# Routed experts: the 48-row rests of the down products side by side in the array, in bursts of four tiles, with three tables of sums

## The reference

```python
# x: 1024 tokens x 256; 16 experts, 4 chosen per token, hidden width 176
shared = silu_and_mul(x @ shared_gate_up_w.T) @ shared_down_w.T   # hidden width 704
shared = shared * sigmoid(x @ sgate_w.T)
topk_w, topk_ids = top_k(softmax(x @ gate_w.T), 4)
for w13_e, w2_e, e in zip(w13, w2, range(16)):
    coef = sum(where(topk_ids == e, topk_w, 0))
    h = silu_and_mul(x @ w13_e.T)          # 256 -> 2 x 176 -> 176
    acc = acc + (h @ w2_e.T) * coef        # 176 -> 256, the down product
out = shared + acc
```

## Time and profile before

| | |
|---|---|
| median of 3 runs | 1252.41 us (1249.12 to 1254.31) |
| profiled execution | 1253.93 us, of which the span from first to last instruction is 1252.0 us |
| first routed stage, first to last up product | 425.11 to 539.58 us |
| second routed stage, the same | 1119.70 to 1233.52 us |
| PE busy | 94% of the span |
| granted TensorE clock, mean | 0.967 of full speed |

### The profile page before, as it was taken

The page is one execution under the profiler, slowest core; times in us unless marked ns, Lnnn a source line. Parts: engine busy times, 40 slices in busy tenths (PEclk is TensorE's granted clock), DMA queues, the critical chain, the costliest instruction groups (busy, mean ns, idle before and its releaser), DMA issues.

```text
span 1252.0 us, 23038 instructions
## 1 busy us (share of the span) xinstructions
PE 1175.0 (94%) x7484; PEld 1008.6 (81%) x7484; DVE 807.0 (64%) x2038; ACT 752.3 (60%) x1734; POOL 600.4 (48%) x497
## 2 busy tenths in 40 slices
PE   6999999999897899989999999999999989489997
PEld 5878888888784777768999999999999988377775
DVE  7766767777882433477777777777777787143335
ACT  5866667666551333427888887887888865033332
POOL 3211222121137165625776777677776643705663
PEclk9999999999997899989999999999999998789999
DMA  3366766653245777741322222232222015556665
GB/s 114 88 181 169 175 174 174 170 162 71 58 153 203 181 137 137 129 103 51 89 77 59 59 61 65 61 70 79 59 75 59 17 48 158 201 168 112 117 116 145
DMA packets 94277, 141.59 MB, mean 113 GB/s; under 512 B 8184, under 2 KB 73976, under 8 KB 93048
## 3 DMA queue, kind: packets, MB, share of 16 engines
q1 hardware_dynamic: 74400, 102.32, 29.8%
q0 software_dynamic: 15744, 20.98, 9.8%
q10 hardware_dynamic: 4056, 17.30, 4.6%
HBM read 99.71 MB, written 40.86 MB: 112 GB/s over the span
## 4 chain that ended last, share of the span: by engine, by line
PE 80%; DVE 6%; DMA 6%; issue 4%; ACT 2%; POOL 1%; SPq 0%; DVEq 0%; ACTq 0%; POOLq 0%
PE ps L276 20%; PE ps L278 19%; PE ps L277 19%; PE ps L1116 7%; PE ps L1141 5%; DMA sums_d<-e_y,xg 3%; PE ps L551 2%; DMA rows_a<-a_rows_d 1%; PE ps L1129 1%; PE ps L1093 1%; DVE valT L762 1%; PE ps L1680 1%; PE ps L565 1%; DMA a_vg_raw<-a_vg 1%; DVE x L1419 1%
## 5 line engine op out<-in xcount | busy, mean ns | idle before, releaser
L1291 POOL DMA_INDIRECT sums_d<-e_y,xg x88 | 137.6, 1564 | 137.2 <-ACT e_y L1218 79.8
L1116 PE MATMUL ps<-w,e_xT 128*128 (+1 forms) x376 | 127.2, 461 | 2.5 <-ACT e_xT L1201 1.7
L1412 DVE COPY e_hT<-ps 88x256 f32<-88x256 f32 x94 | 39.5, 420 | 132.0 <-PE ps L1129 118.0
L427 POOL TENSOR_TENSOR aw_lo<-aw_raw,aw_hi 128x512 fp32r<-128x512 f32 x32 | 42.0, 1317 | 152.5 <-ACT aw_hi L423 152.5
L276 PE MATMUL ps<-xn_hi,aw_hi 128*128 128x512 f32 x256 | 111.2, 434 | 2.7 <-DVE bmat_lo L790 2.7
L857 DVE TENSOR_TENSOR m_a<-ps,e_a 128x384 f32<-128x384 f32 x128 | 71.3, 557 | 58.5 <-PE ps L551 57.9
L278 PE MATMUL ps<-xn_hi,aw_lo 128*128 128x512 f32 x256 | 101.4, 396 | 0.0
L277 PE MATMUL ps<-xn_lo,aw_hi 128*128 128x512 f32 x256 | 100.9, 394 | 0.0
L1141 PE MATMUL ps<-w,e_hT 88*128 (+1 forms) x376 | 96.7, 379 | 0.0
L656 ACT COPY late<-ps 128x256 f32<-128x256 f32 x128 | 47.7, 373 | 69.7 <-PE ps L278 69.6
L427 POOL TENSOR_TENSOR ms_b_lo<-m_b,ms_b_hi 128x384 fp32r<-128x384 f32 x64 | 65.0, 1017 | 49.2 <-ACT ms_b_hi L423 49.2
(11 more groups left out here) (311 smaller groups left out, 4145.8 us busy)
## 6 DMA issues: line engine op xcount, KB each, us to landing
rows_a<-a_rows_d SPq DMA_DIRECT2D x64, 256.0 KB, 5.1
xg<-slots_d SPq DMA_DIRECT2D x94, 144.0 KB
slots_d<-slot_init SPq DMA_DIRECT2D x10, 1152.0 KB, 6.9
w<-moe_up ACTq DMA_DIRECT2D x8, 1408.0 KB
wconv_raw<-b_conv SPq DMA_DIRECT2D x16, 513.0 KB
aw_raw<-a_heads SPq DMA_DIRECT2D x32, 256.0 KB, 3.0
wvo_raw<-b_vo SPq DMA_DIRECT2D x16, 512.0 KB, 3.4
rows_b<-b_rows_d SPq DMA_DIRECT2D x32, 256.0 KB, 4.8
```

The source lines that it names most:

```text
L427: return nc.gpsimd.tensor_tensor(dst[1], src, f32(dst[0]), ALU.subtract).then_inc(sem(done_sem), 1)
L1116: ins = nc.tensor.matmul(ps[:, 2 + t % 2, 0:2 * E_HIDDEN], e_xT[:, t % 2, k], weights_of(w13, t, at_w, k * 2 * E_HIDDEN, 2 * E_HIDDEN), st ...
L1291: nc.gpsimd.indirect_dma_start(sums_d[f][t % CHAINS], bass.IndirectOffsetOnAxis(ap=xg[:, t % XG, ROW_ID:ROW_ID + 1].bitcast(U32), axis=0), ...
L1412: nc.vector.tensor_copy(e_hT[0:HALF_E, t % 2], ps[0:HALF_E, 4 + t % 2, 0:2 * P].rearrange("p (j m) -> p j m", j=2)).then_inc(sem("e_hT"), 1)
```

## The change

- The down product of a tile, 176 rows, is cut into 128 rows (`h_main`) and a rest of 48 (`h_rest`), where it was 88 and 88. The rest of an even tile lies on partitions 0 to 47, that of an odd tile on 64 to 111, so that both can stand in the array at once.
- Down products are no longer done tile by tile but in groups (`DOWN_GROUPS`): nine of four tiles, five of two, and one of one. A group does all its rests, then all its mains. In a group of four, two tiles share a PSUM bank, and one ACT copy takes both out.
- DVE copies the turned hidden values with two instructions, and copies the row numbers of each tile to `e_ids`, so that an `xg` buffer is free as soon as DVE and PE have read it.
- For odd tiles from 16 on, ACT first copies the rest of the down weights to a fixed place (`w_rest`), with a register load of its own.
- PE's register load for tile t+1 stands behind the up product of tile t.
- Three tables of sums instead of two, eight `e_y` buffers instead of four.
- The down weights are laid out on 128 partitions instead of 88.

```diff
+DOWN_GROUPS = [range(t, t + 4) for t in range(0, 36, 4)] + [range(t, t + 2) for t in range(36, TILES - 1, 2)] + [range(TILES - 1, TILES)]
+DOWN_LAG = 2
+E_REST, REST_AT = E_HIDDEN - P, P // 2
-XG, YS, CHAINS, W_GROUPS = 8, 4, 2, 4
+XG, YS, CHAINS, W_GROUPS, HT = 8, 8, 3, 4, 6
...
         def f_experts_pe(pe, f):
-            for t in range(-1, TILES + 2):
+            for t in range(-1, TILES + DOWN_LAG):
                 if t + 1 < TILES:
                     e_turn_pe(pe, f, t + 1)
                 if 0 <= t < TILES:
-                    if t >= EXPERTS:
-                        if t == EXPERTS:
+                    e_up_pe(pe, f, t, at_w)
+                    if EXPERTS <= t + 1 < TILES:
+                        if t + 1 == EXPERTS:
                             routed(pe, "dve", f, "w_at")
-                        at_w[t % 3] = pe.value_load(w_at_i[0:1, t - EXPERTS:t - EXPERTS + 1], min_val=0,
-                                                    max_val=(EXPERTS - 1) * E_STRIDE)
-                    e_up_pe(pe, f, t, at_w)
+                        at_w[t + 1] = expert_at(pe, t + 1)
                 if 0 <= t - 1 < TILES:
                     e_turn_h_pe(pe, f, t - 1)
-                if 0 <= t - 2:
-                    if t - 2 == TILES - 1:
+                for group in due(t):
+                    if group[-1] == TILES - 1:
                         e_last_pe(pe, f, 0)
-                    e_down_pe(pe, f, t - 2, at_w)
+                    e_down_pe(pe, f, group, at_w)
...
+            nc.tensor.transpose(ps[:, 4 + t % 2, 0:P], e_h[:, t % 2, 0:P], ident)
+            nc.tensor.transpose(ps[0:E_HIDDEN - REST_AT, 4 + t % 2, P:2 * P], e_h[:, t % 2, REST_AT:], ident
+                                ).then_inc(sem("e_turned_h"), 1)
...
+        def e_down_pe(pe, f, group, at_w):
+            pe.wait_ge(sem("e_hT"), TILES * f + group[-1] + 1)
+            if group[0] > 0:
+                pe.wait_ge(sem("e_y"), len(READY) * f + ready(group[0]))
...
+            for t in group:
+                r = rest_rows(t)
+                if t >= EXPERTS and t % 2:
+                    pe.wait_ge(sem("w_rest"), MORE_TILES // 2 * f + (t - EXPERTS) // 2 + 1)
+                    w = w_rest[r, t // 2 % (HT // 2)]
+                else:
+                    w = weights_of(w2[r], t, at_w, DM, DM)
+                nc.tensor.matmul(out_of(t, group), h_rest[r, t // 2 % (HT // 2)], w, start=t - group[0] < 2, stop=False,
+                                 skip_group_check=True)
+            for tiles in banks_of(group):
+                for t in tiles:
+                    ins = nc.tensor.matmul(out_of(t, group), h_main[:, t % HT], weights_of(w2, t, at_w, 0, DM),
+                                           start=False, stop=True, skip_group_check=True)
+                ins.then_inc(sem("e_down"), 1)
...
+        def e_rest_act(act, f, t):
+            r = rest_rows(t)
...
+            nc.scalar.copy(w_rest[r, t // 2 % (HT // 2)], w2[r, DM:][:, bass.ds(expert_at(act, t), DM)]).then_inc(sem("w_rest"), 1)
...
+            nc.scalar.copy(e_y[:, n % YS:n % YS + len(tiles)], ps[:, 6 + t % 2, 0:len(tiles) * DM].rearrange("p (i m) -> p i m", m=DM)
+                           ).then_inc(sem("e_y"), 1)
...
+            for n, t in enumerate(ORDER[:POOLED]):
+                pool.wait_ge(sem("e_y"), len(READY) * f + ready(t) + 1)
+                if n >= CHAINS:
+                    added(pool, f, n - CHAINS)
...
+            nc.vector.tensor_copy(e_ids[:, t:t + 1], xg[:, t % XG, ROW_ID:ROW_ID + 1].bitcast(U32)).then_inc(sem("e_row"), 1)
...
-            nc.vector.tensor_copy(e_hT[0:HALF_E, t % 2], ps[0:HALF_E, 4 + t % 2, 0:2 * P].rearrange("p (j m) -> p j m", j=2)
+            turned_h = ps[:, 4 + t % 2, :]
+            nc.vector.tensor_copy(h_main[:, t % HT], turned_h[:, 0:P])
+            nc.vector.tensor_copy(h_rest[rest_rows(t), t // 2 % (HT // 2)], turned_h[REST_AT:E_HIDDEN - REST_AT, P:2 * P]
                                   ).then_inc(sem("e_hT"), 1)
...
-                    added(sp, f, t - XG)
+                    sp.wait_ge(sem("e_row"), TILES * f + t - XG + 1)
+                    sp.wait_ge(sem("e_turned"), TILES * f + t - XG + 1)
...
-            for c in range(CHUNKS):
-                f_last_dve(dve, 1, 0, 0, c)
+            for i in range(CHAINS - 1):
+                for c in range(CHUNKS):
+                    f_last_dve(dve, 1, 0, i, c)
             f_ended_dve(dve, 1, 0, 0)
```

More of the change, by code:

```diff
@@ L1050, in f_down_pe, with banks_of, ready, due @@
                 ins.then_inc(sem("f_down_done"), 1)
+        def banks_of(group):
+            return [[t for t in group if t % 2 == i] for i in range(min(len(group), 2))]
+        READY = [tiles for group in DOWN_GROUPS for tiles in banks_of(group)]
+        ORDER = [t for tiles in READY for t in tiles]
+        def ready(t):
+            return next(n for n, tiles in enumerate(READY) if t in tiles)
+        def due(t):
+            return [group for group in DOWN_GROUPS if group[-1] + DOWN_LAG == t]
         def f_experts_pe(pe, f):
-            at_w = [None] * 3
-            for t in range(-1, TILES + 2):
+            at_w = [None] * TILES
+            for t in range(-1, TILES + DOWN_LAG):
                 if t + 1 < TILES:
@@ L1105, in weights_of, with rest_rows @@
                 return w[:, t * E_STRIDE + first:t * E_STRIDE + first + width]
[L1106 removed]
+            return w[:, first:][:, bass.ds(at_w[t], width)]
+        def rest_rows(t):
+            return slice(t % 2 * REST_AT, t % 2 * REST_AT + E_REST)
         def e_up_pe(pe, f, t, at_w):
@@ L1185, in f_act @@
             routed(act, "dve", f, "w_at")
-            for t in range(-1, TILES + 2):
+            for t in range(-1, TILES + DOWN_LAG + 1):
                 if t + 1 < TILES:
                     e_xT_act(act, f, t + 1)
+                outs = [tiles for group in due(t - 1) for tiles in banks_of(group)]
+                for tiles in outs[:1]:
+                    e_y_act(act, f, tiles)
                 if 0 <= t < TILES:
                     e_silu_act(act, f, t)
-                if 0 <= t - 2:
-                    e_y_act(act, f, t - 2)
+                for tiles in outs[1:]:
+                    e_y_act(act, f, tiles)
+                if EXPERTS <= t < TILES and t % 2:
+                    e_rest_act(act, f, t)
                 if f == 0 and t == POOLED - 3:
@@ L1215, in e_y_act @@
                 return
-            if t >= YS:
-                added(act, f, t - YS)
-            nc.scalar.copy(e_y[:, t % YS], ps[:, 6 + t % 2, 0:DM]).then_inc(sem("e_y"), 1)
+            for i in range(n, n + len(tiles)):
+                if i >= YS:
+                    added(act, f, i - YS)
+            nc.scalar.copy(e_y[:, n % YS:n % YS + len(tiles)], ps[:, 6 + t % 2, 0:len(tiles) * DM].rearrange("p (i m) -> p i m", m=DM)
+                           ).then_inc(sem("e_y"), 1)
         CHAIN = [len(range(q, POOLED, CHAINS)) for q in range(CHAINS)]
@@ L1359, in f_dve @@
                     b_prepare_dve(dve, B_SPLITS.index(t))
-                if t - 2 >= POOLED:
-                    y_last_dve(dve, f, t - 2)
-            y_last_dve(dve, f, TILES - 1)
+            for t in range(POOLED, TILES):
+                y_last_dve(dve, f, t)
         TOKEN_TILE = TILES - CHUNKS * LAST
@@ L2219, in _ @@
             f_dve(dve, 3, 1)
-            for c in range(CHUNKS):
-                f_last_dve(dve, 3, 1, 0, c)
+            for i in range(CHAINS - 1):
+                for c in range(CHUNKS):
+                    f_last_dve(dve, 3, 1, i, c)
             for c in range(CHUNKS):
@@ L2309, in _layout @@
     up = i["L0_ffn_w13"].reshape(EXPERTS, 2 * E_HIDDEN, KT, P).transpose(3, 0, 2, 1)
-    down = np.zeros((HALF_E, EXPERTS, E_STRIDE), np.float32)
-    down[:, :, :2 * DM] = i["L0_ffn_w2"].reshape(EXPERTS, DM, 2, HALF_E).transpose(3, 0, 2, 1).reshape(HALF_E, EXPERTS, 2 * DM)
+    w2 = i["L0_ffn_w2"].transpose(2, 0, 1)
+    down = np.zeros((P, EXPERTS, E_STRIDE), np.float32)
+    down[:, :, :DM] = w2[:P]
+    down[:E_REST, :, DM:2 * DM] = down[REST_AT:REST_AT + E_REST, :, DM:2 * DM] = w2[P:]
     qk = np.stack([i["L0_attn_b_Wq"], i["L0_attn_b_Wk"]]).reshape(2, B_HEADS, B_KD, KT, P)
```

47 lines of the change are left out of this document (27 added, 20 removed).

## The result

The changed kernel took 1269.5 us (median of 5 runs, 1265.6 to 1276.3), the kernel before, measured beside it, 1254.3: ratio 1.014, 95% interval 1.011 to 1.017. On another chip, where before took 1215.7, the ratio was again 1.014 (1.012 to 1.017). The forecast was 1253.2 with a range of 1246 to 1265: wrong by 16 us, and on the side of the third rival, the way over DVE.

The account below looks back on a forecast made before the run. Prediction: PE bounds both loops; loop gains of 4.1 and 3.9 us against stage ends 4.2 and 4.6 longer sum to +0.8, so 1254.7 us profiled, 1253.2 median, range 1246 to 1265.

Parts of the forecast that it names:

- the third rival: In the loops, DVE or ACT binds: bare turns last 1.9 instead of 1.69, +13 us, 1266; chance 12%.
- the way over DVE: Between bursts, copies to `e_h` to next transposes: 1.69 a bare turn from tile 16, 1.4 us a stage.
- The upper bound of 1.78: Bare turn with 0.26 for the new DVE instructions: 3.2 us from tile 16 on, about 1 below.
- PE's own work: From first to last up product, 46 turns and their bursts take PE 108.4 us a stage.
- the burst of four: Down products of four tiles in the loop: 3.0 us, against 3.48 before.
- the change of form: PE's switch into the half array and back, twice a burst: about 0.22 each, 0.43 a burst.
- the end of the second stage: Last burst and added table additions delay the PSUM sums behind the second loop: +4.6 us.
- The first stage's end: DVE decides when the PSUM sums start behind the first loop: +4.2 us.
- the third table: Table additions during the loops: two would bind at 2.38 a tile; the third keeps the gain, brings none.
- Rests in order: Rival on the burst: PE starts in program order, five slots for four rests, +6 us, 1259.2; chance 14%.
- not side by side: Rival on the burst: half-array products run one after another, 9.9 us a stage, 1273; chance 9%.
- changes of form are free: Rival on the bursts: form changes hide, no turn DVE-bound, 7.4 us a stage, 1238, half 1246; chance 13%.

Follow-up runs that it names:

- e2: The changed kernel with only the `e_ids` copy moved behind `e_h` on DVE; one execution took 1262.3 us, loops 112.6.
- e6: e1 with two tables of sums in place of three; one execution took 1212.7 us, 0.997 of the kernel before.
- e8: e1 with odd tiles' rests put on the even tiles' rows, so no two run side by side; loops 117.4 us without the first turns' excess.
- e1: The changed kernel with `e_h` of tile t run on DVE ahead of both copies of tile t-1; 1248.0 us, ratio to before 1.000, on another chip 0.997.
- e7: e1 with down products in bursts of two tiles throughout, not four; loop 111.6 us without the first turns' excess.
- e3: The changed kernel with only the second copy, `h_rest` of tile t-1, moved behind `e_h` of tile t on DVE; one execution took 1249.6 us.
- e5: e1 with the first table added on DVE between the last two `y_last_lo`; 1209.5 us, ratio to before 0.995.
- e4: The kernel before with PE's register for tile t+1 loaded behind the up product of tile t; one execution took 1254.1 us.

## Why the prediction was wrong

The step that failed is the price of the way over DVE. The forecast took 1.52 from the earlier trace rows and added 0.17 for the second copy and the `e_ids` copy together, with 0.26 as the upper bound. Measured are 1.90 and 2.02. The two cost 0.19 (`e_ids`, e2) and 0.18 to 0.30 (the second copy, by the starts above), 0.37 to 0.50 in sum. Below tile 16, where the forecast had 1.61, it was 1.81 and 1.94.

- The row taken for both was the wrong one. The 0.26 is two instructions that belong together, coefficient and its accumulator read, of which the second starts before the first has ended. The trace of before had copies of three sizes (groups of DVE, busy and mean ns of one):

```profile
L1412 DVE COPY e_hT<-ps 88x256 f32<-88x256 f32 x94 | 39.5, 420 | 132.0 <-PE ps L1129 118.0 <-issue 14.0
L1316 DVE COPY lgT<-ps 32x512 f32<-32x512 f32 x2 | 1.4, 679 | 0.3
L1373 DVE CAST e_id<-xg 128x1 f32<-128x1 int32 x6 | 0.9, 147 | 0.0
```

  256 columns more cost 0.26, so some 0.16 of each copy is there whatever its width, and the cast of one column, 0.147, says the same. By these rows the copy split in two costs that fixed part once more (2 x 0.29 for 0.42) and `e_ids` another 0.15: 0.31 of busy time, 0.37 with the pauses. The upper bound of 1.78 was no bound. The Trainium skill, "VectorE: DVE Perf Modes", section "The TRN2 errata — SBUF-src ops pay a fixed extra latency per instruction", has a fixed term too, (N + 151) cycles at 0.96 GHz for a float32 addition. Carried over to copies it gives an estimated 0.291 for 128 columns and 0.158 for one, and the trace agrees: 0.291 and 0.154. I had not set the new instructions against it.
- The loss was also put on the wrong turns. The turn with the burst has its transposes, which wait for `e_h`, ahead of the burst, so it loses as a bare one does; only the turn behind a burst is free. The count of turns per group of four stays three, and one of two in a pair, so this moved little. Below tile 16 the forecast had no loss at all; it was 0.83 for each four tiles, and 1.08 above.
- In sum, by the measured steps, 118.5 - 108.0 = 10.5 a stage where 1.4 (1.9 in the first) had been set: 17.8 us too little in two stages. PE's own work and the first turn had been set 0.5 a stage too high, which leaves 16.7. The point from which the kernel gets slower was named, 1.80 a turn; the third rival's 1.9 gave 1266, and it had 12%. It should have had the most.

What held: the burst of four, 2.98 to 2.99 for 3.0, and that of two, 1.70 for 1.73; rests side by side in full, 0.86 for four; the change of form at 0.40 for 0.43; no idle time at tile 16; PE's work alone 107.97 for 108.4; the end of the second stage +4.7 for +4.6. That last agreement is in part luck: the PSUM sums came 5.1 later than before (15.3 for 10.2 after the start of the last up product), and what follows them was 0.4 shorter. The end of the last up product in the earlier trace rows was also read 0.16 late, since the transposes behind it start at 1234.54. The first stage's end grew by 4.8 for 4.2. Of the third table the forecast gave a wrong reason: e6 shows that two would not have held PE up; they came late at the second stage's end. *Rests in order*, *not side by side* and *changes of form are free* are all excluded, by e8, by the four differences and by the starts:

```profile
475.88 0.48 PE L1176 MATMUL ps<-w,h_rest 48*128 x1
475.89 0.48 PE L1176 MATMUL ps<-w_rest,h_rest 48*128 48x256 f32 x1
476.20 0.38 PE L1176 MATMUL ps<-w,h_rest 48*128 x1
```

The eight records of four rests start in four pairs, at 475.88, 476.20, 476.42 and 476.63. By the rule of the Trainium skill, "TensorE: Matmul & The Clock Gate", section "The mechanism", that matmuls start and end in program order, four rests would have taken five slots of 0.216; the trace has 1.06 with one change of form, four slots and 0.20, and the first pass of an odd rest starts 0.01 behind that of the even one (475.89 and 475.88), ahead of the even one's second (476.20): for two half arrays the trace does not bear out the five slots that I had drawn from the rule.

The sum, put right: the forecast's 1254.7 for the profiled execution, +8.1 and +8.6 for the loops, gives 1271.4 for the 1269.5 measured. What is left over, -1.9, is in the main the start (-1.3) and what lies between the loops (-0.9, the longer end of the first stage included); the second stage's end has +0.1, and the rest is where the second loop is taken to end.

So the gain of the new loop was there, 6.5 and 5.7 us by e1. Of it nine bursts of four give 4.4 (3.48 - 2.99 each) and those of two 0.2; the rest, 1.9 and 1.1, are single longer turns of before that are gone, at tile 16 above all. It was lost to a wait over DVE that the down products had covered, and the ends then cost another 4 to 5 each. e1 takes the wait away by an exchange of two calls and comes out level with before (1.000 and 0.997); with a table added earlier it is 0.5% faster. What stays at the end, 22.6 in e1 for 18.7, has the four additions of the third table, 2.6, as its largest part; but e6 shows that leaving the table out makes the end longer still.

## What to carry to other kernels

When work is gathered into bursts, look first at what it covered where it stood: find the loop over the other engines that is now bare, add it up from start to start, and put each new instruction in at a full slot of its own kind, not at what a fused pair shows. The prices of single instructions there do not add up, since each costs only what the loop then takes beyond the pace of the bounding engine: nothing and 4.6 apart, 10.5 together here. If that loop comes near the pace of the bounding engine, change the order on the other engine so that nothing PE waits for stands behind something PE has only just released. Where a trace has a wait that looks free, check what will stand ahead of it after the change, as in the bank of tile 42.

## What the runs showed of the hardware

- float32 products on 48 of 128 rows, on two halves of the array, ran pairwise without loss: 1.06 for four against 1.92 in a row, each with one change of form. Going from the full array to products on 48 rows or back costs 0.20 each time, independent of how many products follow (e1, e7, e8).
- In the changed kernel a copy of one column took 0.19 on DVE between starts, nearly two thirds of a copy of 128 columns (0.30); in e3 the same copy took 0.08. From the first copy to the coefficient it was 0.34 with one copy of 256 columns, 0.52 or 0.63 with two of 128, by the tile's parity, and 0.21 with one of 128 (e3).
- In e5 PE waited for the router's scatter (busy 3.74 of 7.20), and then ran for some turns at the lower clock level, 1.2 GHz (windows, granted clock in the third column from the right; 0.57 is mostly the lower level):

```profile
1071.30:1078.50 7.20, 3.74 (x12) 1.89 (x13) 2.81 (x12) 1.23 (x4) 2.76 (x3) 0.87 0.63 228
1078.50:1084.20 5.70, 5.70 (x16) 3.83 (x17) 1.43 (x8) 1.07 (x4) 0.00 (x0) 0.57 0.57 159
```

- The kernel before took 1254.3, 1249.5, 1216.8 and 1215.7 us in the four measurements, the last three on three different chips: 3% apart, so only ratios from one chip were compared. By the profiles the difference lies in the main ahead of the routed stages: on the chip of e1 to e4 the first up product stands at 424 to 428 and the way from one loop to the next takes 576 to 585, on the two others 401 to 404 and 556 to 560.
